# Selective scan kernel: C broadcast in pairs, products over two states, state sums in mid-slot, one wait per set of operands, one transfer of B per unit

## The chip, the cores and the metric

The kernel runs on one core of a Trainium2 chip. The metric is the device time of one execution in microseconds (us). TensorE (PE), VectorE (DVE), ScalarE (ACT), GpSimd (POOL) and the DMA queue of SyncE (SP) run side by side, each in the order of its own instruction list, and are tied together by semaphores.

## What is computed

64 series of 750 samples are cut into 10 patches of 128 samples, which gives 640 tokens of width 512. The reference is, cut to what matters:

```
h  = patches @ tok_W.T + tok_b
hn = rmsnorm(layernorm(h))
z, x, B, C, dt_in = split(hn @ in_proj.T)           # 1024, 256, 256, 1024, 128
dt  = softplus(dt_in @ dt_proj.T + dt_b)
dA  = exp(dt * A);  dBx = (dt * x) * B               # 1024 channels x 16 states
s_t = dA_t * s_(t-1) + dBx_t                         # scan over the 10 tokens of a series
y   = (sum over states of C * s + D_skip * x) * silu(z)
h  += out_proj(y)
h  += down(silu(gate(rms(h))) * up(rms(h)))          # 2048 wide
h  += the same with a second set of weights, after layernorm
```

## The kernel before

The tokens are two chunks: chunk 0 with 250 columns, chunk 1 with 390 (`TS`). The 1024 channels are 8 tiles of 128 partitions, the 16 states of a tile are 4 units of 4 states. A chunk is thus 32 units, the program 64. A unit holds its four states in one of four buffers of `hs`. In chunk 0 the scan takes two states in one instruction (`GS` = 2, two pieces a unit, 500 columns), in chunk 1 one state (four pieces, 390 columns).

A unit goes through these steps. SP loads B, broadcast over partitions (`load_b`, L353). POOL multiplies by dt*x (`input_term`, L429). ACT makes the decays exp(dt*A) in two banks of `da` (`decay`, L520). DVE scans (`scan`, L713). PE broadcasts C with a matmul that picks rows (`c_broadcast`, L923) into the two banks of `cps`. DVE multiplies the states by C (`times_c`, L721). POOL adds the halves of the four states (`add_states`, L440 to L452). In chunk 0 PE sums the remaining two states with an identity matrix in float32 (`state_sum`, L934), in chunk 1 POOL does it. DVE makes y (`gate_y`, L730 to L739).

The order is written out by `schedule()`, a list of slots. Every slot has one unit and up to three background steps. In the slots of units 0 to 13 these are the projections of chunk 0 (`dtp`: input of softplus, `in_c`, `xs`, `in_z`), in those of 14 to 19 the token matmuls and norms of chunk 1, from 20 on its projections, and in those of units 32 to 36 the last of these and the output projection of chunk 0. From unit 37 on it is the two MLPs of chunk 0: 32 `gu` steps (a gate product and an up product of 128x250, each four float32 matmuls, which the trace records as eight), and 16 `down` steps. A last slot without a unit has the output projection and the MLPs of chunk 1, whose weights and inputs are split into two float32r parts. ACT and DVE take the background steps of the kinds in `LATE` one slot later than PE, POOL two slots later; a `gu` is in the same slot on all.

Within a slot each engine mixes scan work and background work by `spread(many, few)`. On ACT decays come ahead of background steps. A `gu` there is `Silu` of the gate bank (L651). On DVE a `gu` is one product of the silu with the up bank (L835). The softplus of a tile is five ACT instructions from L636 to L642, DVE's L817, and POOL's L457 and L459; ACT's next softplus waits for POOL's last (`dt_ready`). In `product` (L909) each matmul carries its own wait for its operand.

```
for k, (w, x, *ready) in enumerate(pairs):
    if ready:
        pe.wait_ge(*ready)
    last = nc.tensor.matmul(dst, w, x, start=(k == 0), stop=(k == len(pairs) - 1))
```

A C broadcast of piece k waits for the product of piece k - 2, since `cps` has two banks that take turns.

## Time and profile before

| | us |
|---|---|
| median of 3 runs (793.4 to 797.69) | 796.09 |
| the profiled execution | 794.57 |
| its span, first to last instruction | 792.7 |
| PE busy (2974 matmuls) | 712.0 (90%) |
| POOL busy | 459.6 (58%) |
| DVE busy | 444.4 (56%) |
| ACT busy, 101 table loads in it | 424.6 (54%) |
| mean granted clock of TensorE, as a share of full | 0.944 |

The span is read by stretches. The scan of chunk 0 runs from 31 to 241 us, that of chunk 1 from 241 to 538 us, and the last stage, TensorE with chunk 1's MLPs, from 545 us to the end. The timeline's rows merge equal instructions that follow each other; its first two columns are the start and the time that they took.

### The profile page before, as it was taken

Reading aid. Unit: us, or ns where it says so; the run is one execution under the profiler, and the core shown is the slowest. Engines: PE = TensorE matmul, PEld = TensorE weight load, DVE = VectorE, ACT = ScalarE, POOL = GpSimd, SP = SyncE. Lnnn points to the kernel's source line nnn. Section 1 sums busy time; section 2 is a strip of 40 time slices with the busy share of each in tenths; the row PEclk is TensorE's granted clock in tenths of the full one; section 3 lists DMA queues with packets and bytes.
Section 4 is the critical chain, followed back from the end, with each engine's and each line's share of the span. In section 5 each row is a group of like instructions: output and inputs, shape, how many; then the busy total and the mean of one; then the engine's idle time right before and its main releaser. Section 6 shows DMA issues by size and latency. Waiting matters only on the chain.

```text
span 792.7 us, 9464 instructions
## 1 busy us (share of the span) xinstructions
PE 712.0 (90%) x2974; PEld 545.5 (69%) x2974; DVE 444.4 (56%) x668; ACT 424.6 (54%) x698; POOL 459.6 (58%) x252
## 2 busy tenths in 40 slices
PE   5888886987987697999996999998999999899998
PEld 4655553544544275777674767775699999799998
DVE  4276678667666468787786788783222222322122
ACT  3756667247557445957743973950444343443341
POOL 0475665466656659868767577944445554244551
PEclk9897989999889889999997999999999999999999
DMA  8654441277356253888785588942324333233431
GB/s 352 170 144 106 118 120 51 61 187 226 109 137 162 81 148 97 221 213 228 208 215 142 169 224 224 226 143 83 133 84 140 128 128 116 72 107 110 144 117 42
DMA packets 38049, 116.64 MB, mean 147 GB/s; under 512 B 5360, under 2 KB 15472, under 8 KB 37360
## 3 DMA queue, kind: packets, MB, share of 16 engines
q1 hardware_dynamic: 33648, 110.79, 50.1%
q10 hardware_dynamic: 4352, 5.24, 2.0%
q8 instruction: 25, 0.41, 0.2%
q14 instruction: 24, 0.20, 0.1%
HBM read 108.80 MB, written 7.21 MB: 146 GB/s over the span
## 4 chain that ended last, share of the span: by engine, by line
PE 73%; issue 8%; DVE 8%; ACT 6%; POOL 3%; DMA 1%; SPq 0%; DVEq 0%; ACTq 0%; POOLq 0%
PE work L909 52%; PE da L909 7%; PE c_bcast L923 7%; PE c_bcast L909 4%; PE work L934 3%; DVE hs L713 2%; DVE hs L721 2%; POOL hs L429 1%; POOL hs L440 1%; ACT L495 1%; DVE ysum L734 1%; ACT da L520 1%; ACT L520 0%; ACT pair L636 0%; DMA sm<-small 0%
## 5 line engine op out<-in xcount | busy, mean ns | idle before, releaser
L713 DVE TENSOR_TENSOR_SCAN hs<-da,hs 128x390 f32<-128x390 f32 (+1 forms) x192 | 199.3, 1039 | 18.0 <-DVE gated_n L835 5.7
L520 ACT ACTIVATE da<-dt,a_neg 128x225 f32<-128x225 f32 (+1 forms) x256 | 122.3, 498 | 140.8 <-DVE hs L713 140.1
L429 POOL TENSOR_TENSOR hs<-dtx,bb 128x1000 f32<-128x1000 f32 (+1 forms) x64 | 172.0, 2688 | 14.5 <-DMA bb<-b_rows 11.5
L408 POOL TENSOR_TENSOR ws<-wraw,ws 128x1024 fp32r<-128x1024 f32 x40 | 102.4, 2560 | 112.4 <-ACT ws L528 112.4
L721 DVE TENSOR_TENSOR hs<-hs,c_bcast 128x390 f32<-128x390 f32 (+1 forms) x192 | 111.3, 580 | 72.0 <-PE c_bcast L923 70.9
L440 POOL TENSOR_TENSOR hs<-hs 128x500 f32<-128x500 f32 (+1 forms) x48 | 69.2, 1442 | 123.3 <-DVE hs L721 123.3
L909 PE MATMUL work<-sq,wraw 128*128 128x250 f32 x512 | 128.1, 393 | 2.9 <-DVE sq L788 1.9
L909 PE MATMUL work<-hn,win 128*128 128x250 f32 (+1 forms) x336 | 115.1, 494 | 16.9 <-issue 7.3
L909 PEld LDWEIGHTS work<-sq,wraw 128*128 128x128 f32 x512 | 93.6, 193 | 24.6 <-issue 15.7
L909 PEld LDWEIGHTS work<-hn,win 128*128 128x128 f32 x336 | 69.0, 214 | 48.6 <-issue 18.5
L528 ACT CAST ws<-wraw 128x1024 fp32r<-128x1024 f32 x48 | 50.3, 1048 | 92.5 <-PE work L909 47.1
L923 PE MATMUL c_bcast<-c_st,pick_c 64*128 64x250 f32 (+1 forms) x256 | 84.2, 388 | 10.6 <-DVE hs L721 7.4
L923 PEld LDWEIGHTS c_bcast<-c_st,pick_c 64*128 64x128 f32 x256 | 42.3, 194 | 73.4 <-issue 73.4
L909 PE MATMUL work<-hn,ws 128*128 128x390 f32 x408 | 74.2, 340 | 0.0
L909 PEld LDWEIGHTS work<-hn,ws 128*128 128x128 f32 x408 | 72.6, 188 | 0.0
L909 PE MATMUL work<-gated,ws 128*128 128x390 f32 x336 | 60.7, 341 | 0.0
L909 PEld LDWEIGHTS work<-gated,ws 128*128 128x128 f32 x336 | 60.1, 188 | 0.0
L909 PE MATMUL work<-gated_n,wraw 128*128 128x250 f32 x256 | 58.4, 380 | 0.0
L934 PE MATMUL work<-hs,sm 128*128 128x250 f32 x128 | 39.8, 439 | 20.2 <-DVE ysum L730 12.3
L520 ACT ACT_TABLE_LOAD x43 | 55.2, 1283 | 4.6 <-DVE hs L713 3.8
L909 PEld LDWEIGHTS work<-gated_n,wraw 128*128 128x128 f32 x256 | 47.3, 189 | 8.7 <-issue 3.8
L909 PE MATMUL da<-hn,ws 128*128 128x390 f32 x264 | 49.1, 340 | 2.2 <-DVE hn L873 2.2
(113 smaller groups left out, 787.7 us busy)
## 6 DMA issues: line engine op xcount, KB each, us to landing
wraw<-w_stream SPq DMA_DIRECT2D x104, 512.0 KB, 3.7
bb<-b_rows SPq DMA_DIRECT2D x64, 390.0 KB, 6.1
bb<-b_rows SPq DMA_DIRECT2D x64, 250.0 KB, 4.1
win<-w_in SPq DMA_DIRECT2D x4, 1024.0 KB, 12.9
c_rows<-c_part ACTq DMA_DIRECT2D x8, 390.0 KB, 3.8
c_st<-c_rows SPq DMA_DIRECT2D x32, 97.5 KB, 4.4
c_rows<-c_part ACTq DMA_DIRECT2D x8, 250.0 KB, 3.1
c_st<-c_rows SPq DMA_DIRECT2D x32, 62.5 KB, 3.0
```

The source lines that it names most:

```text
L408: nc.gpsimd.tensor_tensor(ws[:, k % NW, 1, :], wraw[:, split_loads[k] % NRAW, :], ws[:, k % NW, 0, :].bitcast(F32), ALU.subtract).then_inc ...
L429: nc.gpsimd.tensor_tensor(hs[:, u % NH, 0:NQ * n].rearrange("p (n t) -> p n t", t=n), dtx[:, t % 2, 0:n].unsqueeze(1).to_broadcast([P, NQ, ...
L440: nc.gpsimd.tensor_tensor(lo, lo, hi, ALU.add).then_inc(added, 1)
L495: nc.scalar.preload_act_table_set("natural_log_exp_and_others")
L520: last = nc.scalar.activation(dst, src, ACT.Exp, scale=a_neg[:, j:j + 1])
L528: nc.scalar.copy(ws[:, k % NW, 0, :], wraw[:, i % NRAW, :]).then_inc(w_hi_done, 1)
L713: nc.vector.tensor_tensor_scan(flat, da[:, k % ND, 0:w], flat, 0.0, ALU.mult, ALU.add).then_inc(scan_done, 1)
L721: nc.vector.tensor_tensor(flat, flat, cps[:, k % 2, 0:w], ALU.mult).then_inc(c_free, 1)
L734: link(nc.vector.scalar_tensor_tensor(out=y, in0=x, scalar=small_ap(S_DSKIP, m), in1=acc[:, 0:n], op0=ALU.mult, op1=ALU.add))
L909: last = nc.tensor.matmul(dst, w, x, start=(k == 0), stop=(k == len(pairs) - 1))
L923: last = nc.tensor.matmul(cps[:, k % 2, i * n:(i + 1) * n], pick_c[rows, lo:lo + P], c_st[rows, t % NC, q // 2, 0:n], start=True, stop=True)
L934: last = nc.tensor.matmul(work[SUM][:, 0:n], sm[:, S_IDENT:S_IDENT + P], hs[:, u % NH, i * n:(i + 1) * n], start=(q == 0 and i == 0), stop ...
```

## The change

C: `c_broadcast(u, j)` now writes two states, for chunk 1 too, and there it fills both banks of `cps`, so that it waits for the product just before. `times_c` takes two states, 780 columns in chunk 1. PE broadcasts half j = 1 of the unit before at the slot's start and half j = 0 of this unit in mid-slot; the sum of chunk 0 stands ahead of the latter. ACT takes background steps ahead of decays and the `in_z` steps last, with the table of the logarithm behind them. A `gu` of chunk 0 is now `Tanh` of half the gate on ACT, which shares a table with `Exp`, and two DVE instructions. DVE takes `dtp` last in the slot. PE's products wait for an operand only where it is read first. The channels of a tile are permuted (`chan`), so that partitions alternate between the two groups of B and one transfer fills `bb`. The order of the projections in `two_tiles` changes.

```diff
@@ c_pieces -> products
+def products(u):
+    return ([(u - 1, 1)] if u >= 1 else []) + ([(u, 0)] if u < NCH * UNITS else [])
@@ two_tiles
-    return [[("dtp", c, m), ("in_c", c, m)], [("xs", c, m), ("dtp", c, m + 1)],
-            [("in_c", c, m + 1), ("xs", c, m + 1)], [("in_z", c, m), ("in_z", c, m + 1)]]
+    return [[("dtp", c, m), ("in_c", c, m)], [("xs", c, m), ("in_c", c, m + 1)],
+            [("dtp", c, m + 1), ("xs", c, m + 1)], [("in_z", c, m), ("in_z", c, m + 1)]]
@@ load_b (SP)
-                for g in range(2):
-                    src = rows[2 * m + g:2 * m + g + 1, q * w:(q + 1) * w].to_broadcast([64, w])
-                    sp.dma_start(bb[64 * g:64 * g + 64, u % NB, 0:w], src).then_inc(bb_loaded[u % NB], 16)
+                src = rows[2 * m:2 * m + 2, q * w:(q + 1) * w].unsqueeze(0).to_broadcast([P // 2, 2, w])
+                sp.dma_start(bb[:, u % NB, 0:w], src).then_inc(bb_loaded[u % NB], 16)
@@ ACT
-                    silu_tables()
-                    nc.scalar.activation(th[:, i % 2, 0:n], bank(gate), ACT.Silu).then_inc(free_of(gate), 1)
-                    if is_split(s):
+                    if not is_split(s):
+                        tanh_tables()
+                        nc.scalar.activation(th[:, i % 2, 0:n], bank(gate), ACT.Tanh, scale=0.5).then_inc(th_done, 1)
...
-                for s in spread([("decay",) + d for d in decays], stores + steps):
+                for s in spread(others, decays) + z_steps + after:
@@ DVE
+                if GS[c] == 2:
+                    nc.vector.tensor_tensor(half, half, cps[:, k % 2, 0:2 * n], ALU.mult).then_inc(c_free, 1)
+                else:
+                    half = half.rearrange("p (i t) -> p i t", t=n)
+                    nc.vector.tensor_tensor(half, half, cps[:, :, 0:n], ALU.mult).then_inc(c_free, 1)
...
+                        dve.wait_ge(th_done, i + 1)
+                        link(nc.vector.scalar_tensor_tensor(out=gate2[:, 0:n], in0=th[:, i % 2, 0:n], scalar=1.0,
+                                                            in1=bank((s, "gate")), op0=ALU.add, op1=ALU.mult))
+                        dve.sem_inc(free_of((s, "gate")), 1)
+                        full(dve, s)
+                        gated_free(dve, i)
+                        nc.vector.scalar_tensor_tensor(out=gated_n[:, j, :], in0=gate2[:, 0:n], scalar=0.5,
+                                                       in1=bank((s, "up")), op0=ALU.mult, op1=ALU.mult).then_inc(gated_raw, 1)
...
-                    order = spread(parts, others)
+                    order = spread(parts, [s for s in others if s[0] != "dtp"]) + [s for s in others if s[0] == "dtp"]
@@ PE, c_broadcast
-                pe.wait_ge(c_loaded[t % NC], 64 * (t // NC + 1))
+                if q == 0 and j == 0:
+                    pe.wait_ge(c_loaded[t % NC], 64 * (t // NC + 1))
                 if k >= 2:
-                    pe.wait_ge(c_free, k - 1)
+                    pe.wait_ge(c_free, k - 1 if GS[c] == 2 else k)
...
+                for i in range(2):
+                    dst = cps[:, k % 2, i * n:(i + 1) * n] if GS[c] == 2 else cps[:, i, 0:n]
@@ PE, gate_or_up (in_dt, out, down likewise)
+                    ready = [(norm_done, KD * v + k + 1) if first else () for k in range(KD)]
@@ PE, the slots
-                if unit is not None and 2 <= unit < UNITS + 1:
-                    state_sum(unit - 2)
...
+                order = [("c",) + x for x in c_parts[:-1]] + parts[:n]
+                if unit is not None and 2 <= unit <= UNITS:
+                    order.append(("sum", unit - 2))
+                order += [("c",) + x for x in c_parts[-1:]] + parts[n:]
```

How the instructions now stand. First ACT, in a slot of chunk 1 with two `gu` steps: `th` is the result for the gate, `da` the decays, four to a slot. Before:

```order
L651 ACTIVATE th<-work 128x250 [waits bank_full0]
L520 ACT_TABLE_LOAD [waits scan_done]
L520 ACTIVATE da<-dt,a_neg 128x39x9 [waits dt_ready]
L520 ACTIVATE da<-dt,a_neg 128x39x9 [waits scan_done,dt_ready]
L651 ACT_TABLE_LOAD [waits gated_raw]
L651 ACTIVATE th<-work 128x250 [waits bank_full2]
```

and with the change:

```order
L655 ACTIVATE th<-work 128x250 [waits gated_raw,bank_full2]
L523 ACTIVATE da<-dt,a_neg 128x39x9 [waits scan_done,dt_ready] x2
L655 ACTIVATE th<-work 128x250 [waits gated_raw,bank_full0]
L523 ACTIVATE da<-dt,a_neg 128x39x9 [waits scan_done,dt_ready] x2
L655 ACTIVATE th<-work 128x250 [waits gated_raw,bank_full2]
```

The table loads are gone. In both lists two decays stand between two gates, but before, a slot began with two decays and its first gate came behind them, and now a slot begins with the gate: its decays 1 and 2, and again 3 and the next unit's 0, come behind a gate of the same slot.

DVE in such a slot. The scan is printed here as SCALAR_TENSOR_TENSOR hs<-da,hs. Before:

```order
L713 SCALAR_TENSOR_TENSOR hs<-da,hs 128x390 [waits gated_raw,da_done,dbx_done]
L721 TENSOR_TENSOR hs<-hs,c_bcast 128x390 [waits c_full,scan_done]
L713 SCALAR_TENSOR_TENSOR hs<-da,hs 128x390 [waits da_done,dbx_done]
L721 TENSOR_TENSOR hs<-hs,c_bcast 128x390 [waits c_full,scan_done]
L835 TENSOR_TENSOR gated_n<-th,work 128x250 [waits bank_full3,bank_free2]
```

and with the change:

```order
L724 SCALAR_TENSOR_TENSOR hs<-da,hs 128x390 [waits gated_raw,da_done,dbx_done]
L724 SCALAR_TENSOR_TENSOR hs<-da,hs 128x390 [waits da_done,dbx_done]
L736 TENSOR_TENSOR hs<-hs,c_bcast 128x780 [waits c_full,scan_done]
L852 SCALAR_TENSOR_TENSOR pair<-th,work 128x250 [waits th_done]
L857 SCALAR_TENSOR_TENSOR gated_n<-pair,work 128x250 [waits dve_chain,bank_full1]
```

Half a slot is shown. A product now stands behind two scans instead of one.

PE in such a slot. Before:

```order
L923 MATMUL c_bcast<-c_st,pick_c 128x390 [waits c_free,c_loaded1]
L909 MATMUL work<-sq,wraw 128x250 [waits norm_done,bank_free0,w_loaded1]
L909 MATMUL work<-sq,wraw 128x250 [waits norm_done] x3
L923 MATMUL c_bcast<-c_st,pick_c 128x390 [waits c_free,c_loaded1]
L909 MATMUL work<-sq,wraw 128x250 [waits norm_done,bank_free1,w_loaded1]
L909 MATMUL work<-sq,wraw 128x250 [waits norm_done] x3
```

and with the change:

```order
L950 MATMUL c_bcast<-c_st,pick_c 128x390 [waits c_free]
L950 MATMUL c_bcast<-c_st,pick_c 128x390
L933 MATMUL work<-sq,wraw 128x250 [waits bank_free0,w_loaded1]
L933 MATMUL work<-sq,wraw 128x250 x3
L933 MATMUL work<-sq,wraw 128x250 [waits bank_free1]
L933 MATMUL work<-sq,wraw 128x250 x3
```

A pair of broadcasts now stands ahead of a gate and an up product together.

## Rows read from the trace of the kernel before

**Rows 1.** Busy time by stretch: start:end, length, engines, granted clock, DMA share, GB/s

```profile
31.10:118.30 87.20, 71.77 (x244) 49.44 (x245) 59.61 (x75) 55.67 (x124) 55.94 (x43) 0.82 0.51 130
118.30:157.90 39.60, 32.54 (x106) 18.58 (x105) 28.71 (x41) 21.18 (x44) 20.60 (x15) 0.91 0.23 59
157.90:240.90 83.00, 70.54 (x215) 38.63 (x214) 55.49 (x68) 48.98 (x101) 53.34 (x38) 0.92 0.63 167
240.90:308.90 68.00, 50.60 (x156) 30.96 (x155) 42.61 (x65) 36.88 (x59) 45.34 (x26) 0.87 0.44 115
308.90:545.00 236.10, 226.19 (x898) 164.44 (x897) 182.59 (x284) 153.48 (x205) 171.36 (x80) 0.97 0.73 195
545.00:792.70 247.70, 239.20 (x1285) 226.39 (x1283) 66.08 (x115) 94.17 (x136) 107.29 (x45) 0.99 0.34 108
```

**Rows 2.** Instructions by form, 30 to 290 us: busy us, mean ns, idle before

```profile
L713 DVE TENSOR_TENSOR_SCAN hs<-da,hs 128x500 f32<-128x500 f32 x64 | 76.0, 1189 | 7.3 <-ACT da L520 4.8 <-POOL hs L429 2.0 <-DVE hn L780 0.2
...
L721 DVE TENSOR_TENSOR hs<-hs,c_bcast 128x500 f32<-128x500 f32 x64 | 42.3, 661 | 46.8 <-PE c_bcast L923 46.8
L440 POOL TENSOR_TENSOR hs<-hs 128x500 f32<-128x500 f32 x32 | 39.8, 1243 | 67.2 <-DVE hs L721 67.2
...
L459 POOL TENSOR_TENSOR dt<-dt,pair 128x390 f32<-128x390 f32 x7 | 6.5, 933 | 0.5
```

**Rows 3.** Timeline, 220 to 226 us, a softplus and a state sum

```profile
220.22 0.59 ACT L636 ACTIVATE pair<-work,sm 128x390 f32<-128x390 f32 x1
...
222.85 1.95 DVE L817 SCALAR_TENSOR_TENSOR pair<-th,pair 128x390 f32<-128x390 f32 x1 [0.78 <-ACT pair L642]
...
225.82 2.03 PE L934 MATMUL work<-hs,sm 128*128 128x250 f32 x4 [3.50 <-DVE ysum L730]
```

**Rows 4.** Timeline of PE, 318.5 to 323.1 us, one gate and one up

```profile
318.57 0.44 PE L923 MATMUL c_bcast<-c_st,pick_c 64*128 64x390 f32 x1
318.94 1.96 PE L909 MATMUL work<-sq,wraw 128*128 128x250 f32 x8
320.83 0.44 PE L923 MATMUL c_bcast<-c_st,pick_c 64*128 64x390 f32 x1
```

**Rows 5.** Timeline of ACT and DVE in the same stretch

```profile
320.06 0.38 ACT L651 ACTIVATE th<-work 128x250 f32<-128x250 f32 x1
...
321.00 0.41 DVE L835 TENSOR_TENSOR gated_n<-th,work 128x250 f32<-128x250 f32 x1 [1.13 <-PE work L909]
...
321.63 0.97 DVE L713 TENSOR_TENSOR_SCAN hs<-da,hs 128x390 f32<-128x390 f32 x1 [0.21 <-DVE gated_n L835]
...
322.52 0.53 DVE L721 TENSOR_TENSOR hs<-hs,c_bcast 128x390 f32<-128x390 f32 x1
```

**Rows 6.** Instructions by form, 290 to 545 us

```profile
L713 DVE TENSOR_TENSOR_SCAN hs<-da,hs 128x390 f32<-128x390 f32 x112 | 108.1, 965 | 10.7 <-DVE gated_n L835 5.7 <-DVE h L847 2.8 <-ACT da L520 0.8
...
L721 DVE TENSOR_TENSOR hs<-hs,c_bcast 128x390 f32<-128x390 f32 x114 | 61.3, 538 | 4.8 <-PE c_bcast L923 3.8 <-DVE gated_n L835 0.9 <-DVE a L821 0.2
L520 ACT ACTIVATE da<-dt,a_neg 128x351 f32<-128x351 f32 x110 | 60.3, 555 | 78.3 <-DVE hs L713 77.7
...
L651 ACT ACT_TABLE_LOAD x30 | 38.5, 1283 | 0.5
...
L734 DVE SCALAR_TENSOR_TENSOR ysum<-xf,sm,acc 128x390 f32<-128x390 f32 x7 | 11.8, 1684 | 0.0
```

**Rows 7.** Timeline of PE, 206 to 208.7 and 282 to 283.9 us, C in pairs

```profile
206.99 0.49 PE L923 MATMUL c_bcast<-c_st,pick_c 64*128 64x250 f32 x2
...
282.66 0.62 PE L923 MATMUL c_bcast<-c_st,pick_c 64*128 64x390 f32 x2
283.21 0.90 PE L909 MATMUL work<-yg,wraw 128*128 128x250 f32 x3
```

**Rows 8.** Timeline of PE, 584 to 590.6 us, split products

```profile
586.13 4.43 PE L909 MATMUL da<-hn,ws 128*128 128x390 f32 x24
590.40 0.52 PE L909 MATMUL work<-hn,ws 128*128 128x390 f32 x2
```

More of the change, by code:

```diff
@@ L39 @@
 PIECE0 = [sum(UNITS * n for n in NP[:c]) for c in range(NCH)]
-PIECES = UNITS * sum(NP)
+PRODUCTS = NCH * UNITS * 2
 IN_DT, IN_X, IN_B, IN_CZ = 0, 1, 3, 5
@@ L672, in _ @@
                 stores = [("store",) + s[1:] for s in (act_slots[i - 1][1] if i else []) if s[0] == "in_c"]
-                for s in spread([("decay",) + d for d in decays], stores + steps):
-                    if s[0] == "decay":
+                decays, z_steps = [("decay",) + d for d in decays], [s for s in steps if s[0] == "in_z"]
+                others = stores + [s for s in steps if s[0] != "in_z"]
+                after = ["log_tables"] if z_steps and unit is not None else []
+                for s in spread(others, decays) + z_steps + after:
+                    if s == "log_tables":
+                        log_tables()
+                    elif s[0] == "decay":
                         decay(*s[1:])
@@ L879, in _ @@
                     scans = [("scan", unit, p) for p in range(NP[unit // UNITS])]
-                    parts = spread(scans, [("times_c",) + x for x in c_pieces(unit)])
+                    parts = spread(scans, [("times_c",) + x for x in products(unit)])
                     if unit % QU == 1 and unit > QU:
@@ L883, in _ @@
                 if i == len(slots) - 1:
-                    parts = [("times_c",) + x for x in c_pieces(NCH * UNITS)] + [("gate", NCH * KI - 1)]
+                    parts = [("times_c",) + x for x in products(NCH * UNITS)] + [("gate", NCH * KI - 1)]
                 others = []
@@ L993, in step @@
                                 pe.wait_ge(win_loaded[g], 16)
-                    product(s, [(win[:, t, k * P:(k + 1) * P], hn[:, k, 0:n], norm_done, KD * v + k + 1) for k in range(KD)])
+                    ready = [(norm_done, KD * v + k + 1) if kind == "in_dt" else () for k in range(KD)]
+                    product(s, [(win[:, t, k * P:(k + 1) * P], hn[:, k, 0:n], *ready[k]) for k in range(KD)])
                 elif kind == "dtp":
@@ L1007, in step @@
                     pe.wait_ge(w_loaded[i % NRAW], 16 * (i // NRAW + 1))
-                    product(s, [(wraw[:, i % NRAW, m * P:(m + 1) * P], y_of(c, m), y_done, KI * c + m + 1)
-                                for m in range(KI)])
+                    ready = [(y_done, KI * c + m + 1) if s[2] == 0 else () for m in range(KI)]
+                    product(s, [(wraw[:, i % NRAW, m * P:(m + 1) * P], y_of(c, m), *ready[m]) for m in range(KI)])
                 elif kind == "gu":
@@ L1015, in step @@
                     pe.wait_ge(w_loaded[i % NRAW], 16 * (i // NRAW + 1))
-                    product(s, [(wraw[:, i % NRAW, k * P:(k + 1) * P], gated_n[:, k, :], gated_raw, done + k + 1)
-                                for k in range(HH)])
+                    ready = [(gated_raw, done + k + 1) if s[4] == 0 else () for k in range(HH)]
+                    product(s, [(wraw[:, i % NRAW, k * P:(k + 1) * P], gated_n[:, k, :], *ready[k]) for k in range(HH)])
                 elif kind == "down":
@@ L1051, in cols @@
         return v.reshape(n, P).T
+    part, ng = np.arange(P), P // NS
+    group = ng // 2 * (np.arange(ng) % 2) + np.arange(ng) // 2
+    chan = np.concatenate([m * P + NS * group[part % ng] + part // ng for m in range(KI)])
     x = g["x"][:, :, 0]
@@ L1064 @@
     by_state = np.arange(P).reshape(P // NS, NS).T.ravel()
-    order = {s: (s + by_state if c0 <= s < c0 + DI else s + np.arange(P)) for s in starts}
+    order = {s: s + (by_state if c0 <= s < c0 + DI else chan[0:P] if s < DI else part) for s in starts}
     w_in = np.stack([wi[order[s]].T.reshape(KD, P, P).transpose(1, 0, 2).reshape(P, D) for s in starts], 1)
-    row, ch = np.arange(P)[:, None] % 32, np.arange(P)[None, :]
+    row, ch = part[:, None] % 32, chan[None, 0:P]
     pick_x = (row == 16 * (ch // 64) + ch % 16).astype(f)
```

95 lines of the change are left out of this document (52 added, 43 removed).

## Prediction

> **What bounds the kernel now.** I read the busy time by stretch first, because one share for the whole program hides three regimes. The last stretch is TensorE at work 97% of the time (239.2 of 247.7 us). From 309 to 545 us, where chunk 1 is scanned beside the MLP of chunk 0, it is busy 96%. From 31 to 241 us, where chunk 0 is scanned beside projections, no engine reaches 87%, and the granted clock falls to 0.82 to 0.92 [rows 1]. A slot there lasts 87.2 / 14 = 6.2 us, later 83.0 / 12 = 6.9 us, against 2 x (1.19 + 0.66) = 3.7 us of scans and products on DVE [rows 2]. So that stretch is bound by waits that go round.
>
> The groups by form name them: DVE waits 46.8 us for broadcasts of C, POOL 67.2 us for DVE's products [rows 2]. The timeline shows one: L817 starts 2.6 us after the softplus began on ACT and takes 1.95 us, DVE's product and gate stand behind it, and PE's state sum, at the head of its slot with the next broadcasts behind it, starts only after 3.50 us of idle time [rows 3].
>
> In the MLP stretch I go to the timeline of PE: a broadcast, eight matmuls, a broadcast, every 2.26 us, without a gap that anybody else causes [rows 4]. DVE idles 1.13 us there until an up product is done [rows 5]. A gate and an up with their broadcasts take 2 x 2.26 = 4.52 us, by PE alone.
>
> **The change part by part.**
>
> *A gu step of chunk 0 (32 of them).* First PE's own work. From the first of a pair of broadcasts to the next matmul it is 283.21 - 282.66 = 0.55 us [rows 7], where a single one takes 0.37 us [rows 4]. A matmul record within a product takes (1.96 - 0.90) / 5 = 0.21 us [rows 4, 7]. The step becomes 0.55 for the pair, 1.89 for the gate with its turn to what follows, and 8 x 0.21 = 1.70 for the up product, 4.1 us instead of 4.5.
>
> But the pair now fills both banks, so it waits for the product just before. That product stands on DVE behind two scans. The second of them needs a decay that ACT now makes behind the gate of the same half slot (the order of ACT in the section on the change). The next gate on PE stands behind the pair that waits. This is a closed loop, once round for each gu, and I add it up:
>
> - pair to first gate matmul 0.55 [rows 7], the gate's eight matmuls to their end 1.96 [rows 4];
> - 0.10 until a reader starts (the up product, 318.94 + 1.96, ends at 320.90 and DVE starts at 321.00) and 0.38 for the function on ACT [rows 5];
> - decay 0.56 [rows 6], with 0.07 for two hand-overs;
> - scan, start to next start, 322.52 - 321.63 = 0.89 [rows 5];
> - the product of 780 columns, which no row shows: no less than that of 500 columns, 0.66 [rows 2], no more than two of 390, 1.08 [rows 6]. The slope between the two is 0.12 us for 110 columns, which makes 0.97; I take 0.95, and 0.05 until PE goes.
>
> The sum is 5.5 us, with 5.2 and 5.65 as ends. DVE itself needs about 4.0 in it (two scans 1.78, the product 0.95, two instructions for the gate at 0.41 each [rows 5] and 0.2 us of hand-over behind each), so it waits, and PE, at 4.1, waits too. The step goes from 4.5 to 5.5 us, **+32 us** over 32 steps. Every fourth slot has `gate_y` between a product and the next scans: L734 at 1.68 and two more that I put at 0.62 each from the product's row [rows 6] make 2.9 us, the next product ends some 7.1 us behind the one before, 1.6 more than the loop, where the same slots cost about 1 us extra already. **+2 us** for four such slots. If the clock halves in one step out of ten, pair and gate take 2.5 us longer there: up to +8, for the range alone.
>
> *Table loads.* 30 at L651 and about as many before decays leave, 1.28 us each [rows 6], 77 us of ACT. In this stretch ACT idled 77.7 us for scans, so they hid, and I take 0. Had they stayed they would stand in the new loop twice.
>
> *First chunk of the scan.* The sum in mid-slot has half a slot more for POOL's addition, and `dtp` at DVE's end no longer holds up products. What is late next: on ACT a softplus now stands ahead of its slot's decays and still waits for POOL's last softplus. From the end of a scan: the product that POOL waits for 0.6, POOL's addition 1.24 [rows 2], two softplus instructions of about 0.9 each [rows 2], the softplus on ACT 2.6 [rows 3], a decay pair 0.8 (two of the 0.56 kind, less overlap and at 225 columns), then scan 1.2, product 0.6, C's split 0.55, L817 between 0.6 and 1.95 [rows 3], scan 1.2. That is 12 us for two slots, 6.0 a slot against 6.9. With tiles of 250 columns the same sum is about 10.2, 5.1 against 6.2. Floors of a loop are seldom reached while the clock dips, and slots with two `in_z` still give PE and the tables of ACT most to do, so I take half of each difference: 14 x 0.57 = 8 and 12 x 0.45 = 5 us, 2 us for units 14 to 19 and 5 us for the slots at 241 to 309 us, which wait on the same things. **-20 us**, with 0 and -45 (all floors reached and much of the lost clock won back) as ends, and +5 if the new order of ACT hurts.
>
> *Waits in `product`.* Removed are 1032 in the last stage. The records there come every (590.40 - 586.13) / 24 = 0.178 us [rows 8]. Are the waits in that number? Two pairs of broadcasts, of the same float32r, differ by 0.62 - 0.49 = 0.13 us for 2 x 140 columns, 0.46 ns a column, whether or not the second carries a wait [rows 7]; 390 columns at that rate are 0.181 us. The columns alone fill the spacing, and I take 0. The Trainium skill, TensorE: Matmul & The Clock Gate, section Back-to-back issue gap, gives N / 2.4 + 2.5 ns for one matmul behind another, 165 ns here; by that rule 13 ns of each record would be something else, the waits for instance, and 1032 records would give 13 us. The trace's broadcasts do not agree with the rule. The rows leave that way a narrow chance, rival 5.
>
> *At nothing:* one transfer of B instead of two carries the same bytes and is issued two units ahead; POOL idles 67 us for DVE in the first chunk anyway [rows 2]. SP issues 64 fewer, and nothing waits for SP. If that cover is gone it is a microsecond or two each way. The down products keep their pairs of broadcasts, which stood together already.
>
> **Sum.** 794.6 - 20 + 34 = 808.6 for an execution like the profiled one (span 792.7 and 1.9 around it). The median of the runs lies 1.5 above that, so I forecast **810 us**.
>
> **The rivals.**
>
> 1. *The first chunk gains more than the loop costs.* Its place is PE's head of slot, where the sum waits for POOL and DVE; it decides when a slot of the first chunk loses over 34 / 32 = 1.1 us, as at the floors above. With -45: 794.6 - 45 + 34 + 1.5 = 785 us, faster. For it speaks that the clock there stands at 0.82 to 0.92 [rows 1] and rises when PE waits less. Against it: the softplus loop and the long `in_z` slots stay. 0.14.
> 2. *The gate loop does not close*, because decays or products run ahead in a way that I have missed. Then the MLP stretch is PE's own, 32 x (4.5 - 4.1) = -13 us, and with -20 the time is 763 us. For it: it is how the pairing would work if ACT were early. Against it: all links are instruction order and semaphores, not durations. 0.12.
> 3. *The loop closes and the clock falls with it*, or the first chunk gains nothing: 794.6 - 0 + 34 + 8 + 1.5 = 838 us; I put this case at 823 to 840. For it: PE would idle 1.4 us in each 5.5, and the 3.50 us of idle time in rows 3 are followed by matmuls at half pace, 2.03 us for four. Against: the pauses are short. 0.13.
> 4. *It does little of what it says*: the mid-slot sum waits as long as before and the loop is hidden half of the time, within 4 us of 796. 0.04.
> 5. *The waits are in the spacing of the last stage.* A float32 record of 250 columns takes 0.21 us [rows 4, 7]; if a float32r record costs half as much a column, 390 columns are 0.165 us, and 0.013 of the 0.178 belong to something that the change may remove: 1032 x 0.013 = 13 us less, 797 us with the rest as forecast. For it: nearly every record there has a wait. Against it: the slope of the broadcast pairs. The page named above would have it so. 0.05.
>
> **How the numbers follow.** The forecast case has 0.52 and runs from 797 to 823. Half a percent, 4 us, is about what a measurement of this kernel can tell from no change. Of the forecast case 0.05 lies below 800, so slower has 0.47 + 0.13 = 0.60, same 0.05 + 0.04 + 0.05 = 0.14, faster 0.14 + 0.12 = 0.26. The range leaves out rival 2 (0.12) and the outermost part of rivals 1 and 3: 780 to 833.
>
> **What would show it.** In the changed profile: gate products of chunk 0 that start every 5.5 us instead of 4.5, with PE idle before L950 until DVE's L736, and L736's scan released by ACT's decay; PE busy near 80% between 310 and 545 us; a product of 780 columns near 0.95 us; table loads down from 101 to 27; slots of the first chunk at 5.6 to 6.5 us; records of the last stage at 0.178 us and its length unchanged at 248 us. I am wrong if gates come every 4.1 us, if the first chunk ends before 200 us, or if the last stage shortens by over 5 us.

## The result and the profile after

| | before | after |
|---|---|---|
| median of the runs, us | 795.44 (793.4 to 797.69, 4 runs) | 821.23 (810.22 to 825.91, 4 runs) |
| ratio to before, 95% interval | | 1.0229 [1.0139, 1.032] |
| the profiled execution, its span, us | 794.57, 792.7 | 817.28, 815.5 |
| mean granted clock | 0.944 | 0.950 |

The changed kernel is slower: 2.3% by the ratio, clear of no change, though the interval does not settle whether it is above 2%. Two of its four runs, 825.18 and 825.91 us, were slow ones at a lower granted clock and are left out of the ratio, which rests on 810.22 and 817.28. Busy time by stretch of the changed kernel, with the columns of [rows 1]. The borders are again the starts of units 0, 14, 20, 32 and 38; the fifth row ends where the last scan starts, the sixth is the last 248.1 us:

```profile
30.50:107.40 76.90, 60.94 (x243) 43.66 (x244) 57.30 (x74) 52.09 (x121) 56.45 (x43) 0.96 0.47 146
107.40:149.50 42.10, 34.41 (x112) 19.86 (x110) 28.73 (x41) 19.50 (x46) 20.66 (x15) 0.92 0.24 72
149.50:230.60 81.10, 71.14 (x212) 39.38 (x211) 56.64 (x67) 45.21 (x98) 55.41 (x38) 0.89 0.51 169
230.60:299.80 69.20, 47.64 (x147) 30.01 (x148) 44.30 (x54) 28.12 (x51) 43.37 (x25) 0.79 0.30 106
299.80:560.70 260.90, 212.16 (x873) 162.27 (x873) 186.28 (x260) 69.49 (x144) 165.96 (x77) 0.96 0.52 173
567.40:815.50 248.10, 239.58 (x1286) 226.63 (x1284) 66.09 (x115) 94.17 (x136) 107.52 (x45) 0.99 0.34 108
```

Units 0 to 13 took 87.2 us and take 76.9. The MLP stretch takes 260.8 us from unit 38 to the last scan, where it took 229.4 measured in the same way, and TensorE is busy 212.16 / 260.90 = 81% in it, where it was 96%. By stretch the span's 22.8 us are: start -0.6, units 0 to 13 -10.3, units 14 to 19 +2.6, units 20 to 31 -1.9, units 32 to 37 +1.2, unit 38 to the last scan +31.4, the rest +0.4.

These are single executions, and the experiments below tell how far to trust them. Six executions (the changed kernel and e1, e2, e3, e6, e8) have the same lists on ACT, DVE and POOL up to unit 31, and apart from the repeated waits of e3 on PE too. Units 0 to 13 took 76.9 to 82.6 us in them (84.8 in e11, whose lists are the same up to unit 19), units 14 to 19 took 42.0 to 43.4, units 20 to 31 took 75.6 to 82.0, and units 0 to 31 together 195.2 to 204.6. The kernel before and e9, which share theirs, took 209.7 and 211.9 for units 0 to 31. So a difference of a few microseconds in the first chunk between two executions says nothing.

The timeline of the changed kernel in that stretch (start, time taken) shows the loop once round:

```profile
327.93 0.59 PE L950 MATMUL c_bcast<-c_st,pick_c 64*128 64x390 f32 x2 [1.26 <-DVE hs L736]
...
328.45 3.64 PE L933 MATMUL work<-sq,wraw 128*128 128x250 f32 x16
...
330.44 0.38 ACT L655 ACTIVATE th<-work 128x250 f32<-128x250 f32 x1 [4.12 <-PE work L933]
330.71 1.03 ACT L523 ACTIVATE da<-dt,a_neg 128x351 f32<-128x351 f32 x2
331.37 0.97 DVE L724 TENSOR_TENSOR_SCAN hs<-da,hs 128x390 f32<-128x390 f32 x1 [1.51 <-ACT da L523]
...
332.26 0.94 DVE L736 TENSOR_TENSOR hs<-hs,c_bcast 128x780 f32<-128x780 f32 x1
...
333.25 0.62 PE L950 MATMUL c_bcast<-c_st,pick_c 64*128 64x390 f32 x2 [1.16 <-DVE hs L736]
```

The pair at 327.93 lets the gate start at 328.45. ACT's function starts at 330.44, 2.0 us later, halfway through the sixteen matmuls. The decay follows, the scan at 331.37, the product at 332.26, and only then the next pair at 333.25. That is 5.32 us once round; of the intervals between pairs in the stretch, 31 lie at 5.3 to 5.8 us and most of them at 5.35. TensorE did its 16 matmuls by 332.09 and idled 1.16 us.

The waits of the changed kernel, 300 to 560 us (us in total, times, longest):

```profile
ACT th L655 <- PE work L933: 126.8, 30, 6.6
...
DVE hs L724 <- ACT da L523: 50.9, 29, 3.9
PE c_bcast L950 <- DVE hs L736: 44.5, 35, 3.0
```

All three links wait for each other: ACT for the gate, DVE for the decay behind it, PE for the product. No engine in the loop is full. The product itself, by form from 290 to 565 us, takes 942 ns:

```profile
L736 DVE TENSOR_TENSOR hs<-hs,c_bcast 128x780 f32<-128x780 f32 x54 | 50.9, 942 | 0.2 <-PE c_bcast L950 0.2
```

The timeline at units 30 and 32, in the slots of chunk 1's projections, shows what took the place of the waits removed:

```profile
220.33 0.48 ACT L613 CAST c_part<-work 128x390 fp32r<-128x390 f32 x1 [3.89 <-DMA c_rows<-c_part]
...
236.38 4.62 PE L933 MATMUL work<-hn,win 128*128 128x390 f32 x8 [4.96 <-ACT z L629]
...
242.50 0.97 DVE L736 TENSOR_TENSOR hs<-hs,c_bcast 128x780 f32<-128x780 f32 x1 [7.78 <-PE c_bcast L950]
```

`c_part` is a single buffer, and its next use waits for the DMA that empties it. The `in_z` steps, now last on ACT, hold the work tile that PE wants for its next product, and the broadcasts stand behind that product, so DVE waits 7.78 us for them.

### The profile page after: what moved, and what is told of

Same layout as the page of the kernel before. It is cut to its first block, busy times and chain, and to the rows that moved or that the text cites. A ratio compares the mean times of both kernels' runs of the same rounds, so it can differ in the third digit from the quotient of the medians.

```text
span 815.5 us, 8975 instructions
## 1 busy us (share of the span) xinstructions
PE 693.3 (85%) x2974; PEld 543.3 (67%) x2974; DVE 451.8 (55%) x636; ACT 323.0 (40%) x624; POOL 458.3 (56%) x252
## 4 chain that ended last, share of the span: by engine, by line
PE 59%; DVE 16%; issue 9%; ACT 8%; DMA 5%; POOL 2%; SPq 0%; DVEq 0%; ACTq 0%; POOLq 0%
PE work L933 42%; PE da L933 6%; DVE hs L736 5%; PE c_bcast L950 5%; PE c_bcast L933 4%; ACT da L523 4%; DVE hs L724 3%; DMA c_rows<-c_part 3%; PE work L961 2%; DVE ysum L749 1%; DVE pair L832 1%; DVE hs L733 1%; POOL hs L438 1%; ACT L493 1%; DMA bb<-b_rows 1%
## 5 line engine op out<-in xcount | busy, mean ns | idle before, releaser
L724 DVE TENSOR_TENSOR_SCAN hs<-da,hs 128x390 f32<-128x390 f32 (+1 forms) x192 | 197.0, 1039 | 99.3 <-ACT da L523 85.3
L427 POOL TENSOR_TENSOR hs<-dtx,bb 128x1000 f32<-128x1000 f32 (+1 forms) x64 | 171.3, 2678 | 31.2 <-PE work L961 18.3
L933 PE MATMUL work<-sq,wraw 128*128 128x250 f32 x512 | 125.5, 399 | 8.3 <-DVE sq L803 4.5
L950 PE MATMUL c_bcast<-c_st,pick_c 64*128 64x250 f32 (+1 forms) x256 | 72.9, 367 | 55.6 <-DVE hs L736 49.0
L933 PEld LDWEIGHTS work<-sq,wraw 128*128 128x128 f32 x512 | 99.4, 200 | 29.4 <-issue 17.9
L950 PEld LDWEIGHTS c_bcast<-c_st,pick_c 64*128 64x128 f32 x256 | 38.8, 190 | 104.6 <-DVE hs L736 56.5
L933 PEld LDWEIGHTS work<-hn,win 128*128 128x128 f32 x336 | 66.9, 208 | 62.4 <-issue 26.6
L736 DVE TENSOR_TENSOR hs<-hs,c_bcast 128x780 f32<-128x780 f32 x64 | 60.4, 944 | 20.3 <-PE c_bcast L950 20.3
L655 ACT ACTIVATE th<-work 128x250 f32<-128x250 f32 x32 | 12.1, 379 | 126.8 <-PE work L933 126.8
L448 POOL TENSOR_TENSOR acc<-acc,hs 128x780 f32<-128x780 f32 x16 | 29.4, 1839 | 45.2 <-DVE hs L736 45.2
L733 DVE TENSOR_TENSOR hs<-hs,c_bcast 128x500 f32<-128x500 f32 x64 | 41.9, 655 | 21.0 <-PE c_bcast L950 21.0
```

What stands on the lines that cost most here:

```text
L427: nc.gpsimd.tensor_tensor(hs[:, u % NH, 0:NQ * n].rearrange("p (n t) -> p n t", t=n), dtx[:, t % 2, 0:n].unsqueeze(1).to_broadcast([P, NQ, ...
L448: nc.gpsimd.tensor_tensor(total, total, lo, ALU.add).then_inc(added, 1)
L724: nc.vector.tensor_tensor_scan(flat, da[:, k % ND, 0:w], flat, 0.0, ALU.mult, ALU.add).then_inc(scan_done, 1)
L733: nc.vector.tensor_tensor(half, half, cps[:, k % 2, 0:2 * n], ALU.mult).then_inc(c_free, 1)
L736: nc.vector.tensor_tensor(half, half, cps[:, :, 0:n], ALU.mult).then_inc(c_free, 1)
L950: last = nc.tensor.matmul(dst, pick_c[rows, lo:lo + P], c_st[rows, t % NC, q // 2, 0:n], start=True, stop=True)
```

## Experiments

Eleven kernels ran; e1 to e11 are short for them. "Stretches" are always from the start of one unit's first scan to another's, and "to the last scan" is to its start. Medians stand beside the runs of the kernel before on the same chip.

**The loop, cut at ACT (e1).** ACT takes decays ahead of background steps again, in slots with a gate only:

```diff
-                for s in spread(others, decays) + z_steps + after:
+                gate_first = unit is None or not any(s[0] == "gu" for s in steps)
+                mixed = spread(others, decays) if gate_first else spread(decays, others)
+                for s in mixed + z_steps + after:
```

> The changed kernel with one edit: in slots with a gu step ACT takes decays ahead of background steps, as before the change. Theory (closed loop gate - tanh - decay - scan - product - pair of broadcasts - gate, 5.4 us a step): the decay leaves the loop, PE alone bounds the step at 4.1 to 4.3 us, and 32 x 1.2 = 35 us or a little more go: a span of 775 to 785 us where the change has 815.5. Rival A (one set of banks for C is what costs, whatever ACT does): the pair still waits for a product behind two scans, the step stays over 5 us and the span over 805. Rival B (DVE's second instruction for a gate makes DVE the bound): the step stays at 5.0 or more.

Measured: 788.94 us (779.8 to 791.73), ratio to before 0.9895 [0.9817, 0.9974]. TensorE's timeline:

```profile
313.30 0.61 PE L952 MATMUL c_bcast<-c_st,pick_c 64*128 64x390 f32 x2
313.84 3.64 PE L935 MATMUL work<-sq,wraw 128*128 128x250 f32 x16
317.41 0.62 PE L952 MATMUL c_bcast<-c_st,pick_c 64*128 64x390 f32 x2
```

The step is 317.41 - 313.30 = 4.11 us, without a gap, and unit 38 to the last scan takes 227.9 us, 32.9 less than in the changed kernel. As forecast, and both rivals fall: the pair still fills both banks and DVE still has its second instruction. One choice in ACT's order holds the whole loss.

**The loop, lengthened on an engine that idles (e2).** The function of the gate is computed twice, on ACT, which in the changed kernel idles 127 us for it there:

```diff
                         tanh_tables()
+                        link(nc.scalar.activation(th[:, i % 2, 0:n], bank(gate), ACT.Tanh, scale=0.5))
                         nc.scalar.activation(th[:, i % 2, 0:n], bank(gate), ACT.Tanh, scale=0.5).then_inc(th_done, 1)
```

> The changed kernel with the Tanh of a gate issued twice on ACT, the second behind the first's end: 0.40 us more of ACT for each of 32 steps, on an engine that is busy 40% of the time. Theory (closed loop): every step gets longer by just this, 5.4 to 5.8 us, 32 x 0.4 = 13 us in all, a span of 826 to 829. Rivals A and B, in which ACT has no part: nothing, 815 to 817.

Measured: 847.79 us (844.5 to 850.49), 1.0673 [1.0616, 1.0731]. TensorE's timeline:

```profile
334.47 0.59 PE L951 MATMUL c_bcast<-c_st,pick_c 64*128 64x390 f32 x2 [1.67 <-DVE hs L737]
334.98 5.33 PE L934 MATMUL work<-sq,wraw 128*128 128x250 f32 x16
341.38 0.62 PE L951 MATMUL c_bcast<-c_st,pick_c 64*128 64x390 f32 x2 [1.07 <-DVE hs L737]
...
347.15 0.62 PE L951 MATMUL c_bcast<-c_st,pick_c 64*128 64x390 f32 x2 [1.58 <-DVE hs L737]
...
352.92 0.62 PE L951 MATMUL c_bcast<-c_st,pick_c 64*128 64x390 f32 x2 [1.58 <-DVE hs L737]
```

At full clock the step is 5.77 us, 0.42 more than 5.35. ACT's second function starts 0.41 us behind the first (343.92 and 344.33 in the timeline of ACT), so it comes through one for one. But the step from 334.47 took 6.91 us, since part of its matmuls ran at the lower clock (5.33 us for sixteen, not 3.64), and the stretch grew by 29.0 us instead of 32 x 0.42 = 13. Its row of busy time:

```profile
300.00:589.80 289.80, 228.66 (x863) 173.90 (x864) 187.21 (x263) 81.21 (x176) 163.75 (x75) 0.89 0.47 155
```

The granted clock is 0.89 instead of 0.96. The step shows the loop's length, but the span forecast (826 to 829, measured 845.8) missed: the other 16 us go with the clock, in a kernel whose gaps had grown from 1.17 to 1.58 us. It is not the chance of one execution: its four runs have a mean granted clock of 0.918 to 0.925, those of e3 on the same chip 0.942 to 0.952. That the longer gaps lowered the clock is likely but not tested by itself.

**The loop, cut at DVE (e8).** The first product of a half slot goes back between two scans; ACT keeps its new order, C its pairs and its single set of banks:

```diff
+                    if unit >= UNITS:
+                        p = [("times_c",) + x for x in products(unit)]
+                        parts = scans[0:1] + p[0:1] + scans[1:3] + p[1:2] + scans[3:4]
```

> The changed kernel, ACT's gates still ahead of decays, with the loop cut at another link: in chunk 1 DVE takes each product after the first scan of its half slot and not after both, so it no longer waits for the decay behind the gate. Pairs and the single set of banks stay. Theory (closed loop): the step falls to PE's 4.1 to 4.3 us, span 775 to 787. Rival A (the pair on one set of banks costs by itself): 5.0 us or more. Rival B (DVE's work bounds): the same count of DVE instructions, 5.0 us or more.

Measured: 777.59 us (772.22 to 783.02), 0.9796 [0.9736, 0.9857]:

```profile
309.70 0.61 PE L953 MATMUL c_bcast<-c_st,pick_c 64*128 64x390 f32 x2
310.24 3.64 PE L936 MATMUL work<-sq,wraw 128*128 128x250 f32 x16
313.81 0.62 PE L953 MATMUL c_bcast<-c_st,pick_c 64*128 64x390 f32 x2
```

Again 4.11 us. Pairs, one set of banks and gates ahead of decays each stayed, and did no harm with one link gone. The stretch is 220.7 us, 7.2 shorter than with ACT's cut; why, no run separates.

**ACT's order put into the kernel before (e9)**, without pairs:

```diff
-                for s in spread([("decay",) + d for d in decays], stores + steps):
+                decays = [("decay",) + d for d in decays]
+                gate_first = unit is not None and any(s[0] == "gu" for s in steps)
+                for s in spread(stores + steps, decays) if gate_first else spread(decays, stores + steps):
```

> The kernel before with one edit: in the slots with a gu step ACT takes the gate ahead of the decays, as in the changed kernel; Silu with its table loads, single broadcasts in turn on two banks and DVE's order stay. Theory: the loop needs the pair on one set of banks as well. Here a broadcast waits for the product before the last, and from the end of a gate to that product's end it is 2.3 (function, table, decay) + 0.9 (scan) + 0.5 (product) + 0.1 = 3.8 us, against 4.5 us that PE has until the broadcast is due: a gate and an up stay at 4.5 us, the time within 5 us of the kernel before. Rival (ACT's order alone does it): the step gets over 5 us, 16 us or more slower.

Measured: 809.46 us (808.98 to 819.5), 1.0178 [1.0148, 1.0209]. The step came as forecast, the time did not: 14 us more and not within 5. ACT's timeline:

```profile
320.53 0.38 ACT L651 ACTIVATE th<-work 128x250 f32<-128x250 f32 x1 [0.44 <-PE work L911]
320.93 1.28 ACT L520 ACT_TABLE_LOAD   x1
322.22 1.03 ACT L520 ACTIVATE da<-dt,a_neg 128x351 f32<-128x351 f32 x2
323.27 1.28 ACT L651 ACT_TABLE_LOAD   x1
325.04 0.38 ACT L651 ACTIVATE th<-work 128x250 f32<-128x250 f32 x1 [0.48 <-PE work L911]
```

In slots with two gates the step stays 4.51 us, even with two table loads in it. So ACT's order alone does not close the two-gate loop. Of the 25.5 us that its MLP stretch lost, 13 lie in three slots with a single gate: unit 46 takes 10.3 us instead of 6.7, unit 48 12.1 instead of 8.5, unit 55 12.4 instead of 6.6. There all four decays of a unit stand behind the one gate, with the table loads. The clock has a part in it: around units 46 and 55 it is 0.72 (382 to 397 us) and 0.69 (477 to 499 us). This execution is also the slowest of the five, 9 us above the next, so some of the 25.5 is its own. In the changed kernel, which has no table loads here, these slots lose less (7.1, 9.2 and 8.0 us). In the median, gates ahead of decays thus cost 14 us without any pair, by another way than the one that I forecast.

**The waits in `product` (e3)**, each matmul with its own again:

```diff
-                    ready = [(norm_done, KD * v + k + 1) if first else () for k in range(KD)]
+                    ready = [(norm_done, KD * v + k + 1) for k in range(KD)]
```

and five lines like it.

> The changed kernel with each matmul of a product waiting for its operand again. Theory (the columns fill the spacing, waits that are met cost nothing): records of the last stage stay at 0.178 us, the last stage at 248 us, the time within 2 us of the changed kernel. Rival (waits are in the spacing and something else in the change took the gain): the last stage gets longer, by up to 13 us.

Measured: 821.53 us (816.56 to 823.62), 1.0335 [1.0281, 1.0389]. From the last scan's start to the end it is 254.8 us, as in the changed kernel. In the last stage of the two kernels, first this one:

```profile
611.15 4.43 PE L933 MATMUL da<-hn,ws 128*128 128x390 f32 x24
615.42 8.70 PE L933 MATMUL work<-hn,ws 128*128 128x390 f32 x48
```

then the changed kernel:

```profile
608.86 4.43 PE L933 MATMUL da<-hn,ws 128*128 128x390 f32 x24
613.13 8.70 PE L933 MATMUL work<-hn,ws 128*128 128x390 f32 x48
```

Both give 4.27 / 24 = 0.178 us a record, as in [rows 8]. A wait that is met already costs no time here; the edit is worth nothing either way. What does fill the 0.178 us, the columns or something else, this run does not tell.

**The sum back at the slot's head (e4):**

```diff
-                    order.append(("sum", unit - 2))
+                    order.insert(0, ("sum", unit - 2))
```

> The changed kernel with the state sum of chunk 0 back at the head of PE's slot. Theory (the sum in mid-slot is what sped up the first chunk, 87.2 to 76.9 us over units 0 to 13, by not holding the next broadcasts): units 0 to 31 take 8 to 15 us more. Rival (the gain came from DVE taking dtp last, or from ACT's order): under 3 us.

Measured: 824.18 us (816.49 to 827.48), 1.0364 [1.0297, 1.043]. Units 0 to 31 take 210.2 us; it was 209.7 in the kernel before and 200.1 in the changed one. Against the 195.2 to 204.6 us of the six executions with the sum in mid-slot, its place is worth 5 to 15 us and accounts for the gain of the first chunk. PE's and POOL's waits, 30 to 240 us, with the sum at the head:

```profile
POOL hs L438 <- DVE hs L733: 68.8, 21, 8.6
...
PE work L961 <- POOL hs L438: 11.0, 7, 5.5
```

and in the changed kernel, where PE's products and sums no longer wait for that addition:

```profile
POOL hs L438 <- DVE hs L733: 47.1, 20, 4.8
PE work L933 <- DVE c_part L826: 17.7, 10, 2.7
...
PE work L933 <- ACT z L629: 12.3, 6, 5.0
```

It shows also what was late next: `c_part` and the `in_z` steps.

**ACT's whole order as before (e7)** (decays first, `in_z` not last):

```diff
-                decays, z_steps = [("decay",) + d for d in decays], [s for s in steps if s[0] == "in_z"]
-                others = stores + [s for s in steps if s[0] != "in_z"]
-                after = ["log_tables"] if z_steps and unit is not None else []
-                for s in spread(others, decays) + z_steps + after:
+                for s in spread([("decay",) + d for d in decays], stores + steps):
```

> The changed kernel with ACT's whole order of before: decays first, in_z not last, no early table of the logarithm; Tanh, pairs, mid-slot sums and DVE's order stay. Theory: the loop is gone in the MLP stretch (step 4.1 us); unit 32, where broadcasts stand behind an in_z product whose bank ACT frees last (12.8 us against 8.2 before), is back near 8 us; the first chunk keeps what the sum in mid-slot gave, within 4 us. Span 766 to 776. Rival: ACT's new order is what sped up the first chunk, which then takes 8 us or more longer, span over 780.

Measured: 783.39 us (781.24 to 785.62), 0.9869 [0.9827, 0.9912]. The span is 781.7 us, above the 766 to 776 forecast. Units 0 to 13 take 75.7 us, no more than in any execution of the changed kernel's lists, so the new order of ACT did not bring the first chunk's gain. Unit 38 to the last scan takes 229.9, since the loop is cut here too. Unit 32 falls from 12.8 to 10.4 us, but unit 33 rises from 9.8 to 13.9: the wait for `in_z` only changes slots, and the 4 to 5 us forecast for it did not come.

**The order of tiles as before (e5):**

```diff
-    return [[("dtp", c, m), ("in_c", c, m)], [("xs", c, m), ("in_c", c, m + 1)],
-            [("dtp", c, m + 1), ("xs", c, m + 1)], [("in_z", c, m), ("in_z", c, m + 1)]]
+    return [[("dtp", c, m), ("in_c", c, m)], [("xs", c, m), ("dtp", c, m + 1)],
+            [("in_c", c, m + 1), ("xs", c, m + 1)], [("in_z", c, m), ("in_z", c, m + 1)]]
```

> The changed kernel with two_tiles in the order of before (dtp and in_c, xs and dtp, in_c and xs, in_z twice), so that in_c steps are two slots apart and not one. Theory: in the changed kernel ACT waits 18 us for the store of c_part, the one buffer that two in_c steps in a row share, and PE waits behind it; the first chunk (units 0 to 31, 200 us) gets 5 to 12 us shorter. Rival: the softplus loop binds these slots, and two dtp in a row are worse: it gets longer by 3 us or more.

Measured: 814.07 us (812.2 to 819.24), 1.0266 [1.022, 1.0313]. Units 20 to 31 take 73.4 us instead of 81.1, units 0 to 19 take 2.8 us more; for units 0 to 31 together it is 4.8 less, just short of the 5 to 12 forecast. With `in_c` in two slots that follow each other, the second waits for the buffer of the first. For chunk 1 this shows: the three kernels with the old order there (e5, e10, e11) take 73.4 to 73.8 us, the six with the new one 75.6 to 82.0, so it costs 2 to 9 us. For chunk 0 nothing is shown: 121.8 us for units 0 to 19 lies within the 118.9 to 126.6 that the new order took.

**Decays first in chunk 1 from unit 37 on, not only beside gates (e6):**

```diff
-                for s in spread(others, decays) + z_steps + after:
+                gate_first = unit is None or unit < UNITS + 5
+                mixed = spread(others, decays) if gate_first else spread(decays, others)
+                for s in mixed + z_steps + after:
```

> The changed kernel with decays ahead of background steps on ACT from unit 37 on, so also in the slots of the norms, 37 and 51. Theory: beside the closed loop (the step at 4.1 us, as in e1, span 778), the norm of unit 37 holds the decays in the changed kernel, which makes its slot 15.5 us against 11.7 before; it goes back to about 12, span 774 to 776. Rival: the norm's slot is longer because gate_y on DVE now stands ahead of the norm, whatever ACT does: 777 to 779.

Measured: 789.98 us (781.92 to 794.82, 10 runs), 0.9929 [0.9897, 0.9962]. This missed: the span is 789.7 us, and not 774 to 776. Units 0 to 13 alone, whose lists did not change, took 82.6 us at a granted clock of 0.82, 5.7 more than in the changed kernel. Unit 37 still takes 15.5 us, where it took 11.7 before; ACT's order is not its cause. In the changed kernel its timeline has

```profile
293.39 3.48 DVE L749 SCALAR_TENSOR_TENSOR ysum<-xf,sm,acc 128x390 f32<-128x390 f32 x1
...
298.60 6.66 PE L933 MATMUL work<-sq,wraw 128*128 128x250 f32 x16 [4.45 <-DVE sq L803]
```

DVE makes y ahead of the norm for which PE waits to begin the MLP. The kernel before has y ahead too (L734 at 303.15 us, the norm at 307.09), and PE waited 1.94 us there. The sixteen matmuls behind the wait take 6.66 us here and not 3.64, at a granted clock of 0.54 (298.6 to 305.3 us), which lands in unit 38.

**The parts put together (e10, e11).** First the product between scans with the old tile order for chunk 1 alone (`if c == 0` keeps the new one).

> e8 (the product between the scans) with chunk 1's tiles in the order of before, chunk 0's in the new one. Theory: the two gains lie in different stretches and add up. e8 has a span of 774, and units 20 to 31 took 7.7 us less in e5; units 0 to 19 were better with the new order: span 764 to 769. Rival: the slots at units 32 to 36 give it back: 771 or more.

Measured: 774.18 us (769.33 to 777.01), 0.9727 [0.9684, 0.9771]: units 20 to 31 73.4 us, unit 38 to the last scan 220.6, both gains kept. The span forecast missed (775.2 us, not 764 to 769): units 0 to 13, whose lists did not change, took 81.2 us instead of 76.9. Then unit 37's y behind the norm too:

```diff
+                    if unit == UNITS + QU + 1:
+                        order = [s for s in order if s[0] != "gate"] + [("gate", unit // QU - 1)]
```

> e10 with gate_y of unit 37 on DVE behind the norm of that slot and not ahead of it. Theory: in unit 37, 15.5 us whatever ACT does (e6, e7), PE waits 4.45 us for the norm, which stands behind a gate_y of 4.7 us; 3 to 4 us less than e10. Rival: the norm's own chain from ACT binds it: less than 1 us.

Measured: **768.87 us (765.41 to 776.5), 0.968 [0.9621, 0.9738]**. PE's wait for the norm falls from 4.57 us to 0.32, and units 37 and 38 together take 21.0 us instead of 25.2, where 3 to 4 less was forecast. Units 51 and 52 fell from 24.5 to 18.3 us and unit 47 grew from 7.7 to 11.4, but the edit changes no list there: the clock does, 0.57 against 1.00 in the first pair of stretches (419 to 430 us in e10, 421.2 to 427.7 in e11) and 0.50 in e11 at 374 to 379.6 us. The medians lie 5 us apart with overlapping runs, and the two profiled spans are 775.2 and 774.7, so in the whole time this last step is not shown; the local gain is. Either version beats both kernels.

## Why the prediction was right, and where its sizes were off

**The gate loop: right.** Forecast was 5.5 us with 5.2 and 5.65 as ends; the trace has 5.32. Its links in the timeline above are 2.51 from the pair to the function (forecast 2.61), 0.93 to the scan (1.01), 0.89 to the product (0.89), and 0.99 until the next pair (1.00). The product of 780 columns, which no row of before had, was taken at 0.95 and takes 0.94. The MLP stretch was forecast at +34 and measured +31.4.

The total came nearer than its parts. The loop took less than the +32: in this stretch 27 pairs ahead of a full gate and up product lie 5.33 to 5.78 us apart, 5.39 on average, which against 4.51 is 24 us. About 3 us, which the forecast did not have, are the sixteen matmuls at 298.60, which take 6.66 us at a granted clock of 0.54 and not 3.64; they make unit 38 13.0 us instead of 8.2, of which two steps of the loop explain 1.7.

The +2 for `gate_y` came near by other sizes. The next product starts 5.53 us behind the one before (342.97 and 348.50 in the timeline of DVE), not 7.1, and that is DVE's own work end to end: `gate_y` takes 1.7 us there and not 2.9, since L749 takes 0.62 where the forecast took the mean 1.68 of L734 (the last section says what is in that mean). Units 41 and 61 have a `down` step in that half slot and not a gate, and the pairs lie 5.53 and then 4.13 us apart, where they lay 4.13 and 4.48 apart: 1 us more each. The other 2 to 3 us are spread, and I have not separated them.

Cutting the loop at either of two links gives the 4.11 us of TensorE alone (forecast 4.1), and lengthening it gives what was added. That is rival 2's step, reached by taking away what it said was not there; its -13 us for the stretch did not come in full (-1.5 and -8.7).

**The first chunk: right in sign, under half the size.** The term of -20 measured -8.4, as follows.
- Units 0 to 13: forecast -8, measured -10.3. Seven more executions of the same lists give -2.4 to -10.3, so the size fits and the exact figure is luck. The sum's place accounts for the gain up to unit 31.
- Units 20 to 31: forecast -5, measured -1.9, and -1.0 to -7.5 over the six executions. "Slots with two `in_z` still give PE and the tables of ACT most to do" named the wrong thing: it is the second `in_c`, which waits for its single buffer. With the old tile order it is 73.4 us, or -9.6.
- Units 14 to 19: forecast -2, measured +2.6, and at least +2.3 in every execution. With the sum at the slot's head they take still longer, 47.9 us. I have no run that explains the rest; it stays open.
- Slots at 241 to 309 us: forecast -5, measured +1.2. That they "wait on the same things" failed. Unit 32 waits for `in_z`, now late on ACT (ACT's old order only moves that wait to unit 33), and unit 37 for a norm behind `gate_y`, as the last kernel shows. I priced `gate_y` against the loop and not against the norm.

The working took the softplus loop as what is late next. The waits name `c_part` and `in_z` instead (17.7 and 12.3 us on PE), so that part of the mechanism was wrong where its sizes came out.

**Waits in `product`: right.** Forecast 0, measured 0; rival 5 falls. The rule of the Trainium skill, TensorE: Matmul & The Clock Gate, section Back-to-back issue gap, gives 165 ns for 390 columns; the records come every 178 ns with and without the repeated waits. The trace does not agree with it, and the difference is not waits. The page calls this the gap of an isolated matmul and says that for large N it over-counts a real stream; here it under-counts one. The prediction's own reason, that the columns alone fill the spacing, rests on the slope of the broadcast pairs and is not shown by the run with the waits repeated.

**Table loads: right.** 27 remain of 101, and those removed had hidden behind ACT's waits. In the kernel before with gates first on ACT, two of them stand in every two-gate step, and it stays at 4.51 us. What they would cost in the closed loop no run shows.

**Clock.** The stretch kept 0.96, so the +8 held for the range alone did not come; about 3 us did, ahead of unit 38. In the kernel with the function twice such a cost was there, and larger (16 us).

**Sum.** 794.6 - 8.4 + 31.4 - 0.6 + 0.4 = 817.4, the profiled execution. It lies 9 us above the 808.6 forecast for it: 11.6 that the first chunk did not give, less 2.6 that the MLP stretch did not take. The median of the four runs is 4 us higher still. Their scatter goes with the mean granted clock: 810.22 us at 0.962, 817.28 at 0.950, 825.18 at 0.938, 825.91 at 0.932. What sets the clock of a run, no run here explains. Part of the closeness is luck: a first chunk priced too well stands against a loop priced too dear.

**Rivals 1 and 3.** The first chunk gave 8.4 us and not the 34 that rival 1 needs. Rival 3 is not as far off: in the profiled execution the clock held in the stretch of the loop, but two of the four runs lie in its band of 823 to 840 us, at the lowest clocks, and a first chunk that gives little was one of its conditions.

## What to carry to other kernels

Each engine's list can look harmless while four together close a loop: gate, decay, scan, product, broadcast, gate. Before moving a step, write the chain from one use of a single buffer to the next across all engines, add it up with rows of the trace, and compare it with the busiest engine's own work. If it is longer, cut one link; two were tried here, and either did, worth 33 and 40 us. An engine that idles most of the time can still be in such a loop, and then each of its nanoseconds counts.

A kernel with the same lists can differ by several microseconds in one stretch from one execution to the next. Before a small difference is given to an edit, look at stretches that the edit does not touch, and at the granted clock in them.

A wait that moves somewhere else has to be followed to the next single buffer. The sum in mid-slot was worth 5 to 15 us, and 2 to 9 were lost to `c_part` until the steps that use it stood two slots apart.

## What the runs showed of the hardware

- Semaphore waits already met cost a stream of float32r matmuls nothing: 0.178 us a record of 390 columns with and without.
- In the kernel with the function twice, TensorE idled 1.67 us ahead of a pair, and the sixteen matmuls behind took 5.33 us instead of 3.64, at a granted clock of 0.77 over 334 to 341.4 us. The stretch had 0.89 at a step of 5.77 us. At a step of 5.35 us it held 0.96 in the changed kernel and 0.99 in three more (e3, e4, e5).
- DVE's L749, 390 columns, ran eight times in the changed kernel. Five times no POOL instruction was under way, and it took 0.62 or 0.63 us. Three times it started while POOL's L427 ran; it took 3.48, 2.34 and 2.35 us, and each ended 0.42 us after POOL's did. In the kernel before, the same instruction (L734) started beside a POOL one seven times of eight, took 1.28 to 2.32 us and ended 0.42 or 0.43 us after it; that is the mean of 1.68 that the forecast used. The timeline of the changed kernel:

```profile
293.24 3.21 POOL L427 TENSOR_TENSOR hs<-dtx,bb 128x1560 f32<-128x1560 f32 x1
293.39 3.48 DVE L749 SCALAR_TENSOR_TENSOR ysum<-xf,sm,acc 128x390 f32<-128x390 f32 x1
...
340.43 3.23 POOL L427 TENSOR_TENSOR hs<-dtx,bb 128x1560 f32<-128x1560 f32 x1
...
343.83 0.62 DVE L749 SCALAR_TENSOR_TENSOR ysum<-xf,sm,acc 128x390 f32<-128x390 f32 x1
...
418.46 3.23 POOL L427 TENSOR_TENSOR hs<-dtx,bb 128x1560 f32<-128x1560 f32 x1
...
419.77 2.34 DVE L749 SCALAR_TENSOR_TENSOR ysum<-xf,sm,acc 128x390 f32<-128x390 f32 x1
```

The first of these stood ahead of the norm in unit 37, so part of that unit's 15.5 us is this one instruction. Not every DVE instruction beside POOL is slowed: the scan at 342.08 lies beside the POOL instruction at 340.43 and takes its usual 0.97 us. Over the whole trace the division is by where the operands lie. The softplus's L832, 390 columns, reads two tensors in SBUF like L749; it takes 0.55 to 0.56 us alone and 1.57 to 2.82 us when it starts beside POOL (four times each). Scans, products by C and the `gu` instructions read one operand from PSUM (`da`, `cps`, `work`): the 79 scans of 390 columns that start beside POOL take at most 0.97 us, like the others. So the 1.95 us of L817 in [rows 3] was this too, and not the instruction's own length.
